# A fused SSM and butterfly FFN block on one core: new order of work in the first two phases and the last, and fourteen weight loads on another queue

## What is computed

```python
x = x + ssm(layernorm(x))          # in_proj to x and z (512 each), causal conv of 4 taps, silu,
                                   # x_proj to delta, B(16), C(16); delta = softplus
    h = h * exp(d_t * A) + x_t * d_t * B_t     # over 2048 steps, state 512 x 16
    y_t = h @ C_t;  y = (y + x_conv * D) * silu(z);  out_proj to 256
x = x + ffn(layernorm(x))          # W_exp to 1024, butterfly of 10 stages, + up_bias, gelu,
                                   # butterfly of 10 stages, W_con to 256, + b_con + down_bias
```

## Time and profile before

| | us |
|---|---|
| median of 3 runs | 561.27 |
| lowest, highest | 560.69, 564.58 |
| the profiled execution | 566.98 |
| its span, first to last instruction | 564.9 |
| TensorE busy | 521.1 (92%) |
| VectorE busy | 414.1 (73%) |
| ScalarE busy | 307.9 (55%) |
| GpSimd busy | 91.4 (16%) |

### The profile page before, as it was taken

One profiled execution on the slowest core, in us unless ns is written; L12 is line 12 of the kernel. 1 busy time (PEld: TensorE's weight loads), 2 busy tenths in 40 slices (PEclk: granted clock), 3 DMA queues, 4 the chain that ended last, 5 costly groups with the idle time before them and its releaser, 6 DMA issues.

```text
span 564.9 us, 8225 instructions
## 1 busy us (share of the span) xinstructions
PE 521.1 (92%) x3012; PEld 427.4 (76%) x3012; DVE 414.1 (73%) x892; ACT 307.9 (55%) x537; POOL 91.4 (16%) x88
## 2 busy tenths in 40 slices
PE   4986899799999999999999999999999999769987
PEld 3764676576788888887888789778888887658876
DVE  4858999657994899489966997599848784645532
ACT  3766883656128751785259623972287418621342
POOL 4040200320011300150013201320113001210110
PEclk9987988979999999999999999999999999889999
DMA  9543311200021101210112001200111011100011
GB/s 231 112 27 5 77 38 38 62 16 1 2 75 39 39 2 37 75 41 0 39 38 77 1 16 62 70 8 2 37 44 35 2 38 40 38 1 0 1 38 37
DMA packets 42635, 21.75 MB, mean 39 GB/s; under 512 B 26435, under 2 KB 41027, under 8 KB 42596
## 3 DMA queue, kind: packets, MB, share of 16 engines
q1 hardware_dynamic: 39956, 17.57, 13.0%
q10 hardware_dynamic: 2640, 3.67, 2.3%
HBM read 16.78 MB, written 4.46 MB: 38 GB/s over the span
## 4 chain that ended last, share of the span: by engine, by line
PE 50%; DVE 19%; ACT 11%; issue 10%; SPq 6%; POOL 2%; DMA 1%; ACTq 0%; DVEq 0%; POOLq 0%
PE acc L872 11%; PE wide L861 10%; PE wide L850 9%; PE wide L710 8%; DVE xc L1490 5%; SPq L424 5%; PE wide L824 4%; DVE state L1595 3%; PE wide L835 2%; ACT xc L1160 2%; PE small L700 2%; DVE diag_sum L1613 2%; DVE diag L1609 2%; DVE hid_low L1507 1%; ACT L1160 1%
## 5 line engine op out<-in xcount | busy, mean ns | idle before, releaser
L1120 ACT ACTIVATE hid_f<-wide,bias_up 128x512 f32<-128x512 f32 x64 | 43.9, 686 | 169.7 <-PE wide L861 166.4
L1490 DVE SCALAR_TENSOR_TENSOR xc<-xi,taps,xc 128x512 f32<-128x512 f32 x96 | 83.7, 877 | 4.6 <-ACT xc L1151 2.3
L872 PE MATMUL acc<-w_down_high,hid_high 128*128 128x256 f32 x256 | 73.0, 285 | 3.1 <-DVE hid_low L1507 3.0
L872 PE MATMUL acc<-w_down_high,hid_low 128*128 128x256 f32 x256 | 72.0, 281 | 0.0
L872 PE MATMUL acc<-w_down_low,hid_high 128*128 128x256 f32 x256 | 72.0, 281 | 0.0
L1507 DVE TENSOR_TENSOR hid_low<-hid_f,hid_high 128x512 fp32r<-128x512 f32 x64 | 45.5, 714 | 30.4 <-ACT hid_high L1233 30.0
L530 POOL TENSOR_TENSOR rstd<-var_eps,minus_half 128x4 f32<-128x4 f32 x16 | 19.7, 1233 | 286.9 <-DVE var_eps L1396 286.9
L710 PE MATMUL wide<-xnT_ln1T_high,w_in_high 128*128 128x512 f32 x128 | 57.3, 448 | 6.1 <-ACT xc L1151 3.2
L861 PE MATMUL wide<-xnT_ln2T_high,w_up_high 128*128 128x512 f32 x128 | 55.1, 430 | 4.9 <-DVE xnT_ln2T_low L1501 4.9
L850 PE MATMUL wide<-w_out,xc 128*128 128x256 f32 x256 | 58.5, 388 | 0.9 <-DVE xc L1657 0.5
L850 PEld LDWEIGHTS wide<-w_out,xc 128*128 128x128 f32 x256 | 49.2, 195 | 8.2 <-issue 1.5
(11 more groups left out here) (193 smaller groups left out, 1048.1 us busy)
## 6 DMA issues: line engine op xcount, KB each, us to landing
x_res<-in_L_attn_x_dram SPq DMA_DIRECT2D x9, 512.0 KB, 3.5
c_near<-c_of_tokens SPq DMA_DIRECT2D x8, 512.0 KB
x_ln<-in_L_attn_x_dram SPq DMA_DIRECT2D x7, 512.0 KB, 3.6
out_dram<-x1b_xn SPq DMA_DIRECT2D x7, 512.0 KB, 2.9
xc<-in_L_attn_in_proj_w_dram ACTq DMA_DIRECT2D x2, 512.0 KB, 6.7
xc<-in_L_ffn_W_exp_dram ACTq DMA_DIRECT2D x1, 1024.0 KB, 11.9
x1b_xn<-in_L_ffn_W_con_dram ACTq DMA_DIRECT2D x1, 1024.0 KB, 15.3
raw_out<-n_L_attn_out_proj_w_dram ACTq DMA_DIRECT2D x1, 512.0 KB, 7.7
```

The costliest lines, as they stand in the source:

```text
L872: last = pe.matmul(acc[:, c, :], hid[h][:, j % HRING, c * P:(c + 1) * P], w_down[w][:, j, 0:DM], start=j == 0 and c % 2 == 0 and n == 0, s ...
L1120: ins = act.activation(out_ap, in_ap, how.pop("func"), **how)
L1490: ins = dve.scalar_tensor_tensor(xc[u % BATCH][:, e, :], xi[:, e, tap:tap + TILE], taps[:, e, tap:tap + 1], xc[u % BATCH][:, e, :], ALU.mu ...
```

## The change

- `load_low(act, DOWN, down_weights)` replaces `load_low(sp, DOWN, down_weights)`: the 14 loads stand on ScalarE's queue behind W_con.
- SP issues `spread_c(0)` ahead of `load_for_norm(2)`.
- Phase 0: PE transposes unit 1 (`ln1T`) between `prepare(4)` and `prepare(5)`; ACT takes its high parts there, ahead of scaling; DVE takes the low parts ahead of `multiply_short_paths`.
- Phase 1: `scale_blocks(UP, 2)` comes after the high parts of `ln2T`, `prepare(15)` after `z 5`.
- POOL: the residual of unit u - 1 comes after `b_with_c` and waits for the last gate of unit u.
- Phase 7: PE runs `up 3` before y, then `down 2`, `up 4`, the second half of y, `down 3`, `up 5`, `down 4`, both output projections, `up 6`, `down 5`, `up 7`, the transposes of unit 7, `down 6` and `down 7`. ACT makes two gelus instead of three ahead of the second exp table. DVE assembles before it advances the state, and takes the low parts of unit 7 before it finishes unit 6.

```diff
-            load_low(sp, DOWN, down_weights)
...
+            spread_c(0)
             load_for_norm(2)
-            spread_c(0)
...
             for u in range(UNITS):
-                if u:
-                    residual_with_bias(u - 1)
...
                 if u + 2 < UNITS:
                     rstd_of(u + 2, 0, var1, rstd1)
+                if u:
+                    wait(pool, gated, u, CB)
+                    residual_with_bias(u - 1)
                 rstd_of(u, 1, var2, rstd2)
...
                 prepare(4)
+                transposes(1, "ln1T", x_ln, norm1)
                 prepare(5)
                 prepare(6)
-                transposes(1, "ln1T", x_ln, norm1)
...
+            def last_outputs(u):
+
+                p = u - 1
+                ssm_output_halves(u, 0)
+                down(p, 2)
+                up(p, 4)
+                ssm_output_halves(u, 1)
+                down(p, 3)
+                up(p, 5)
+                down(p, 4)
+                out_projection(u, 0)
+                out_projection(u, 1)
+                up(p, 6)
+                down(p, 5)
+                up(p, 7)
+                transposes(u, "ln2T", xn2, norm2)
+                down(p, 6)
+                down(p, 7)
...
             act.dma_start(raw_con, W_con.rearrange("(g p) d -> p g d", p=P)).then_inc(w_loaded["con"], 16)
+            load_low(act, DOWN, down_weights)
...
                 prepare(4)
+                high_parts(1, "ln1T")
                 prepare(5)
+                place_halo(1)
                 scale_blocks(DOWN, 0)
-                place_halo(1)
-                high_parts(1, "ln1T")
...
-                beside("abs")
                 if v == UNITS:
                     load_gelu_table()
-                    for j in range(3):
-                        gelu(p, j)
+                    gelu(p, 0)
+                    gelu(p, 1)
                     load_exp_table(2)
...
                 softplus(0)
+                low_parts(1, "ln1T")
                 multiply_short_paths(UP)
                 sum_biases()
-                low_parts(1, "ln1T")
...
+            def to_last_outputs(u):
+
+                p = u - 1
+                diagonal_times_c(u)
+                sum_diagonal(u)
+                assemble(u)
+                low_hidden(p, 2)
+                advance_state(u)
+                gates_of_halves(u, 0)
+                low_hidden(p, 3)
+                gates_of_halves(u, 1)
...
+                if v == UNITS:
+                    low_parts(u, "ln2T")
                 final(p)
```

More of the change, by code:

```diff
@@ L1027, in last_ffn @@
             def last_ffn(u):
-                transposes(u, "ln2T", xn2, norm2)
                 for j in range(HB):
@@ L1296, in phase @@
                     high_parts(p, "ln2T")
+                    beside("ln2T")
                 if v < UNITS:
@@ L1306, in phase @@
                     copy_z(v, 5)
+                beside("z 5")
                 take_c_start(u)
                 exp_diagonal(u)
-                beside("diagonal")
                 if v < UNITS:
@@ L1334, in weights_of_ffn @@
             def weights_of_ffn(place):
-                if place == "abs":
+                if place == "ln2T":
                     scale_blocks(UP, 2)
-                elif place == "diagonal":
+                elif place == "z 5":
                     prepare(15)
```

41 lines of the change are left out of this document (22 added, 19 removed).

## The result

The changed kernel takes 583.26 us (median of 4 runs, 582.01 to 585.97); the kernel before, run beside it, 562.13 us (4 runs). The ratio is 1.038, with a 95% interval from 1.032 to 1.043: slower by 3.8%, about 21 us. The forecast was 572, with a range up to 581: the direction was right, the size was not, and the time lies 2 us outside the range.

A forecast was written before the change was run, and what follows sets the result against it. TensorE bounds phases 2 to 6 (150 to 470 us), VectorE 60 to 90 us; room is at both ends. +31 - 4 - 8 - 8.5 = +10.5 us on the 561.27 median: 572 us, range 549 to 581.

The forecast's parts named there:

- Term 1: Start: fourteen down_weights loads issued on ScalarE's queue delay its first compute and everything after, by 31 us.
- D: Start: time ScalarE spends issuing the fourteen down_weights loads, delaying all that follows; taken as 31 us.
- Term 2: Phase 0: unit 1's high parts ahead of scaling end VectorE's 3.70 us wait; 4 us gained (2 to 5).
- Term 3: Phase 1: residual behind the gates, scaling behind the high parts; 8 us gained (4 to 10).
- Term 4: Phase 7: new order shortens TensorE's 5.33 us wait before m_mat's products; 8.5 us gained (5 to 10).
- The residual beside the convolutions and C's spread: Phases 2 to 6: residual costs nothing, at worst 0.4 us per phase; phase 0: spread's moved DMAs nothing, within 1 us.
- The first: Start: issues hold ScalarE no longer than the median issue says, 8.3 us; 549 us; chance 0.15.
- the second: Start: ScalarE held as SP was by the down set, 16.3 us, to 20; 557, up to 561; chance 0.17.
- the fourth: Phase 7: TensorE bound by low parts in their new places, gain only 4 us; 576 us; chance 0.06.
- The third: Start: SP and ScalarE wait for each other, 37.6 us; 588 us, or 578 with expected gains; chance 0.12.

The follow-up runs named there:

- the first experiment's version: The changed kernel with one line undone, the fourteen down_weights loads back on SP's queue: 546.35 us, ratio 0.969.
- the version with the spread ahead: The changed kernel with the down loads back on SP and C's spread of unit 0 put ahead of those loads: 545.85 us, ratio 0.966.

## Why the prediction was right in direction and wrong in size

**Term 1, the size of D: this step failed.** That ScalarE computes nothing while it issues, that its own queue fills behind the large loads, and that phases 2 to 6 carry the loss to the end, all held. D was taken as 31 us, "the row of the nearest case plus about a third of that overlap", with 37.6 as the upper end "if these wait in full for each other". They do wait in full: 38.95 us on the trace, above even that upper end, and 36.7 to 38.4 us in the time, by how the medians are paired. The choice of a third rested on no row. The rows at hand bore the right sum: 27.32 and 16.30 us for the two sets on one queue are 43.6 us of work, and if both queues share what drains them, both end near 5.1 + 43.6 = 48.7 us; ScalarE's ended at 47.2. The step treated the second queue as mostly extra capacity and only its tail as shared, and the reading of the earlier trace rows helped in that: one long issue among thirteen short ones looked like a single obstacle. The experiment that split it moved the waiting to its neighbours: the longest issue fell from 9.6 to 5.8 us and the hold only from 39.66 to 35.33. Counting the clock after TensorE's rest as nothing did hold: granted 0.86 from 50 to 100 us, and 0.86 too in the same stretch of the first experiment's version, from 11.2 to 61.2.

**Term 2: this failed too, behind a number that looks right.** Phase 0 gained 3.8 us on the trace (forecast 4), but 3.4 of them are there in the kernel with the loads moved alone, where the down weights had long landed. The new order adds 0.4. That the number agrees is luck. Even the 3.4 are set against a slow execution of the kernel before: by medians the loads alone cost 36.7 us at a D of 37.4 (45.69 - 8.25), which leaves 0.7. With the loads back on SP the named wait of 3.70 us goes and another comes, VectorE's for C near, 2.35 us in one execution and 4.79 in another, and no gain is seen at the first mark.

**Term 3.** Phase 1 was forecast at 8 and showed 9.8 up to unit 6 between the two profiled executions. With the loads on SP it is 6.6 us for the order and 2.3 for the residual in phase 1, 8.9 together: this term held, with the waits that it names (3.21 us, the normalise's 2.1). How much of it is the clock was not separated. By medians phases 0 and 1 are worth 6.5 to 8.0 and the residual 2.0, so 8.5 to 10 where the sum had 12 and, for the residual in phase 7, another 0.5; term 2 is what is missing.

**Term 4.** Measured from the last sum into the output of phase 6, the out projection starts 38.4 us later instead of 43.0 and the last FFN 55.8 instead of 64.1; the forecast had 38.4 and 56.1. Between the two profiled executions phase 7 gained 9.1 us (forecast 8.5); by medians 6.9, and 2.0 more with the residual in all phases. Waits of 0.83, 0.76 and 2.11 us stood for about 1, 1 and 2.3.

**The residual beside the convolutions and C's spread** cost nothing that can be seen in phases 2 to 6: TensorE is busy 307 of 310 us there, and from one sum of the diagonal to the next (units 2 to 6) it is 59.6 us in both kernels.

**The sum.** Forecast +31 - 20.5 = +10.5 us. By medians +36.8 - 17.2 = +19.6, and measured +21.1 (the kernel before at 562.13 instead of the 561.27 of the forecast adds another 0.9 to the time). Six microseconds are D, the largest error; three are gains that were not there, mostly those of term 2. The rest, under 2.5 us, is within the scatter of the medians. With D alone put right the forecast would have been 578 to 580, inside the range.

**The rivals.** The first (D under 20.5) and the second (D as the down set's 16.3) are refuted by ScalarE's rows at the start of the profile after; the fourth by the 0.83 us and by the 6.9 us for which phase 7 was priced. The third had the right D (37.6) and an interval (578 to 588) that holds the result; it had a chance of 0.12 where the rows deserved it as the likeliest. Its mechanism, that SP and ScalarE wait for each other, is half right. ScalarE's fourteen take 24.38 us alone and 39.66 beside SP's, so they do wait for each other. They don't do so as the rival had it, with SP's long issue holding ScalarE's: in the changed kernel three of ScalarE's issues end while SP's is held from 8.40 to 27.27 us, and with long pieces thirteen pass while it is held from 8.89 to 23.84. The Trainium skill, "Perfetto Trace Analysis", section "DMA Instruction — HWDGE (DVE, Sync)", has one issuer lock the descriptor generator until its descriptors are made, with the lock wait inside the shown time. That last part fits (ScalarE's median issue is 2.5 us beside SP's set); a lock kept all through SP's held issue does not, by both traces.

The rule of "DMA: Bandwidth & Descriptors", section "Issuing engines are not separate DMA queues", in the same skill, was right where it was against this change (a second issuer adds no DMA engine: the two sets take 42.4 us at once and 44.7 one behind the other) and wrong in the half by which D would have been small: 39.66 us is issue time here.

## What to carry to other kernels

Loads of hundreds of 8-byte pieces hold the engine that issues them, here for 16 to 40 us a set. Another engine's queue hardly shortened the sum of two sets (42.4 us instead of 44.7), so keep such loads on an engine that computes nothing, and price both sets as one sum. A single long issue in a row of short ones need not be the cause of the waiting: split, it moved the waiting to the others. A wait that is gone is a gain only if no other stands behind it: look for the next one in the same stretch. Measure gains at an end of the kernel against several executions, not against the one that was profiled.

## What the runs showed of the hardware that was not expected

- Fourteen loads of 4 KB, 57 KB in all, hold an issuing engine 39.66 us in 8-byte pieces beside a like set, 24.38 us alone behind the large loads, and 8.46 us as contiguous rows beside a set in 8-byte pieces.
- The total of two sets is 41.5 to 44.7 us, on one queue, on two at once, or one after the other on two. Cut into 44 loads instead of 28, from 5.16 to 42.87 us, it is 37.7.
- An issue of another engine can end while one is held: with long pieces in 0.26 to 0.61 us each, with 8-byte pieces in 2.8 to 4.6 us each. What inside the chip holds them stays open: the number of pieces, or what few partitions do to them. No run measured one issue alone with a known number of pieces before it.
- Loads into two and four partitions, cut into single partitions, raise the DMA share from 0.22 to 1.04 and move the same 4 GB/s.
- POOL at work beside VectorE: eight additions of 128x256 from 4.10 to 6.21 us, a normalise from 1.39 to 3.4, one instruction of four columns from 0.17 to 2.25.
- The last stage, behind the last sum of the diagonal, takes one of two times. Ten of the profiled kernels have the new order of phase 7: in five the stage takes 61.9 or 62.0 us at a granted clock of 0.99 to 1.00, in the other five 63.3 to 63.5 at 0.97. Here are the first experiment's version and the version with the spread ahead:

```profile
481.00:545.00 64.00, 55.88 (x344) 48.74 (x342) 31.06 (x55) 20.47 (x32) 6.99 (x3) 0.97 0.05 17
```
```profile
481.00:543.00 62.00, 54.05 (x341) 47.10 (x339) 30.74 (x55) 20.16 (x32) 6.99 (x3) 1.00 0.05 18
```

With the 2.4 us by which the wait for C near varied, that is about the size of the scatter between runs of one kernel, 545 to 549.5 us; it also says that a difference of 1.5 us at the end of one trace is no price. Why the profiled execution of the kernel before lay 4.9 to 5.7 us above its medians was not traced to its cause.
